# The last layer of a four-layer image kernel turned round: transposes behind the gate, interleaved patches, border columns moved by DMA

## The reference

```python
hidden = conv1x1(x, w_in)                      # 48 -> 288 channels
# patches of 8 x 8: rfft2, times fft_mask, irfft2
hidden = depthwise 3 x 3 (hidden, w_dw)        # 288 channels, zero padding
a, b = split(hidden)                           # 144 and 144
out = conv1x1(gelu(a) * b, w_out)              # 144 -> 48, added to x
```

## Time and profile before

| | |
|---|---|
| time, median of 3 runs | 12465.18 us (12453.49 to 12465.48) |
| profiled execution, span | 12461.3 us (the page has no other time of it) |
| TensorE busy in the span | 97% |
| the last layer | from about 9431 us to the end, 3030 us |

### The profile page before, as it was taken

The page is one execution under the profiler, slowest core; times in us unless marked ns, Lnnn a source line. Parts: engine busy times, 40 slices in busy tenths (PEclk is TensorE's granted clock), DMA queues, the critical chain, the costliest instruction groups (busy, mean ns, idle before and its releaser), DMA issues. The chain is left out here.

```text
span 12461.3 us, 389987 instructions
## 1 busy us (share of the span) xinstructions
PE 12084.7 (97%) x160850; PEld 8648.5 (69%) x160850; DVE 7757.3 (62%) x17493; ACT 5633.1 (45%) x11858; POOL 4999.7 (40%) x4364
## 2 busy tenths in 40 slices
PE   8999999899989999899999999999998999999999
PEld 7877444499977777555555555555557888888887
DVE  0000455444435545788888888888887777777777
ACT  0000111243433333455555555555556777777776
POOL 0000222212420055566666666666663444444444
PEclk9999999999999999999999999999999999999999
DMA  4333465695984587766666666666662222222222
GB/s 142 132 132 132 127 159 154 147 179 89 166 164 146 147 230 199 93 88 87 88 89 88 88 88 88 88 88 87 89 87 67 57 57 57 57 54 56 55 55 52
DMA packets 2289545, 1323.30 MB, mean 106 GB/s; under 512 B 1876085, under 2 KB 2199164, under 8 KB 2202256
## 3 DMA queue, kind: packets, MB, share of 16 engines
q1 hardware_dynamic: 2013196, 1200.80, 49.5%
q10 hardware_dynamic: 275072, 105.14, 3.7%
HBM read 648.82 MB, written 450.45 MB: 88 GB/s over the span
## 5 line engine op out<-in xcount | busy, mean ns | idle before, releaser
L1803 PE MATMUL l_m<-l_wa,l_pix 128*128 128x288 f32 x8192 | 2211.4, 413 | 2.7 <-DVE l_wb L1985 2.7
L1803 PEld LDWEIGHTS l_m<-l_wa,l_pix 128*128 128x128 f32 x8192 | 1475.5, 190 | 688.8 <-issue 361.9
L1659 POOL TENSOR_TENSOR l_qkv<-l_qkv,l_copies 128x576 f32<-128x576 f32 x1024 | 1437.1, 1403 | 631.3 <-DVE l_qkv L1996 621.5
L1649 POOL TENSOR_TENSOR l_pix<-l_raw 128x516 f32<-128x516 f32 x1024 | 1217.1, 1189 | 1042.6 <-DVE l_t L2033 1017.1
L1484 PE MATMUL l1h_ps<-l1h_ring,l1h_w 96*96 96x256 f32 x6120 | 1328.8, 379 | 62.7 <-ACT l1h_ring L1426 60.2
L1484 PEld LDWEIGHTS l1h_ps<-l1h_ring,l1h_w 96*96 96x96 f32 x6120 | 999.8, 163 | 391.5 <-issue 60.4
L2318 PEld LDWEIGHTS l_e<-k_ident,l_turn 128*112 128x112 f32 x9900 | 1069.1, 133 | 173.0 <-issue 110.6
L2318 PE MATMUL l_e<-k_ident,l_turn 128*112 128x128 f32 x9900 | 1158.2, 275 | 11.4 <-ACT l_turn L2403 3.0
L2403 ACT ACTIVATE l_spread<-l_e 112x512 f32<-112x512 f32 (+1 forms) x1584 | 871.7, 569 | 521.4 <-PE l_e L2318 509.5
L1517 DVE SCALAR_TENSOR_TENSOR l1h_ring<-l1h_ps,l1h_bias,l1h_columns 96x256 f32<-96x256 f32 x1020 | 670.4, 657 | 678.4 <-PE l1h_ps L1484 672.7
L517 PE MATMUL l0a_rows<-l0a_x 128*49 128x245 f32 x8144 | 1043.0, 371 | 0.0
(11 more groups left out here) (269 smaller groups left out, 22947.3 us busy)
## 6 DMA issues: line engine op xcount, KB each, us to landing
l0a_x<-x_px_dram SPq DMA_DIRECT2D x128, 1176.0 KB, 5.1
l0b_x<-x_in_dram SPq DMA_DIRECT2D x128, 493.8 KB
l_raw<-l_raw SPq DMA_DIRECT2D x128, 483.6 KB, 7.3
l_raw<-x_dram SPq DMA_DIRECT2D x1270, 48.0 KB, 3.7
l_x<-x3p_dram SPq DMA_DIRECT2D x132, 384.0 KB
l_out<-x_dram SPq DMA_DIRECT2D x528, 96.0 KB, 2.4
out_dram<-l_out SPq DMA_DIRECT2D x132, 384.0 KB, 4.5
x_dram<-l0b_out ACTq DMA_DIRECT2D x256, 193.5 KB, 3.1
```

What stands on the lines that cost most here:

```text
L1649: nc.gpsimd.tensor_tensor(pix[:, n % 2, i, half * HALF:(half + 1) * HALF].rearrange("p (r w) -> p r w", w=PW), in0, in1, op).then_inc(pix_ ...
L1659: nc.gpsimd.tensor_tensor(q, q, copies[:, g % 2, 1:2, :].broadcast_to([128, 2, OUTC]), ALU.add)\
L1803: last = nc.tensor.matmul(bank[i][:, 0:OUTC], pix[:, k, i, first:first + 128], wa[:, b, i, :], start=True, stop=(i in (1, 2)))
```

## The change

Gelu, gate and border adds now work on `turn`, before any transpose: patches on the partitions, positions and channels along the free side. Only the gated product (`gate`) is transposed, 16 times per third, into `rows`; the projection reads `rows`, with four positions of a patch at four places of 32 partitions each. `turn` exists twice.

The two images of a slab are interleaved on the partitions (patch t of image s at 2t + s), so that the neighbour of a patch lies two partitions on. Since neighbours no longer share a partition, `move_edges` sends the outer columns of a third to them, with two transfers of 126 partitions on SyncE's queue; GpSimd clears the two lanes at the seam of the channel halves, waits for the transfers, adds the columns to `turn`, and adds and saves the rows as before. The projection of slab n - 1 is one piece behind convolution 1 of slab n. Channel order in the constants is natural again.

```diff
-            def join(pairs):
-                s = spread[:, pairs]
-                nc.gpsimd.tensor_tensor(s[:, :, 8, :, 0:TX - 1], s[:, :, 8, :, 0:TX - 1], s[:, :, 0, :, 1:TX], ALU.add)
-                nc.gpsimd.tensor_tensor(s[:, :, 1, :, 1:TX], s[:, :, 1, :, 1:TX], s[:, :, 9, :, 0:TX - 1], ALU.add)
...
+                    pool.wait_ge(a_out, conv_at(n, j, COMP))
+                    pool.wait_ge(b_out, conv_at(n, j, COMP))
...
+                    nc.gpsimd.memset(turn[HI:HI + 2, u % 2, 0], 0.0).then_inc(parted, 1)
+                    pool.wait_ge(edge_in[u % 2], 32 * (u // 2) + 32)
...
+                    nc.gpsimd.memset(edge[HI:HI + 2, u % 2, 0], 0.0).then_inc(ended_edge, 1)
+                    nc.gpsimd.tensor_tensor(tile[:, 1:9:7], tile[:, 1:9:7], edge[:, u % 2], ALU.add).then_inc(edged, 1)
...
+            def move_edges(n, j):
+                u = n * 3 + j
+                sp.wait_ge(a_out, conv_at(n, j, COMP))
+                sp.wait_ge(b_out, conv_at(n, j, COMP))
+                if u >= 2:
+                    sp.wait_ge(edged, u - 1)
+                here, there = slice(0, 126), slice(2, 128)
+                for side, column, dst, src in ((0, 9, there, here), (1, 0, here, there)):
+                    if side == 1:
+                        sp.wait_ge(parted, u + 1)
+                    sp.dma_start(edge[dst, u % 2, side, :],
+                                 turn[src, u % 2, column].rearrange("p y g i -> p (y g i)")).then_inc(edge_in[u % 2], 16)
...
+                move_edges(n, 0)
+                move_edges(n, 1)
                 if not first:
-                    store(n)
+                    store(n - 1)
+                move_edges(n, 2)
...
+            def transpose(n, j, ended):
...
+                    if i % 2 == 0:
+                        pe.wait_ge(gate_out, u * 2 + 1 + i // 2)
+                    for k in range(4):
+                        group = 4 * i + k
+                        last = nc.tensor.transpose(bank[:, k * 128:(k + 1) * 128],
+                                                   gate[:, u % 2, 4 * group:4 * group + 4, :].rearrange("p m i -> p (m i)"),
...
+            def project(n, ended):
+                pe.wait_ge(t_out, n * 12 + 12)
...
+                for k in range(6):
+                    j, r = k // 2, k % 2
+                    for m in range(4):
+                        lanes = slice(m * LANE, m * LANE + CH)
+                        for side in range(2):
+                            last = nc.tensor.matmul(e[m][side * HI:side * HI + C, :], wout[lanes, j, r, :],
+                                                    rows[lanes, j, side * 8:(side + 1) * 8, r, :], start=(k == 0), stop=(k == 5),
...
+            def gelu(u, h):
+                if h == 0:
+                    act.wait_ge(edged, u + 1)
+                    act.wait_ge(carried, u + 1)
+                nc.scalar.activation(half(u, 0, h), half(u, 0, h), ACT.Gelu).then_inc(gelu_out, 1)
...
+                        if g < 2 and n > 0:
+                            pe.wait_ge(f_out, n * 4 - 2 + 2 * g)
```

More of the change, by code:

```diff
@@ L2108, in stage_l3 @@
     BANDS = H // 8 + 1
+    N = 2 * BANDS
     CH = C // 2
@@ L2116, in stage_l3 @@
     AB = YR + 3 * COMP
[L2117 to L2125, removed]
+    EDGE = 10 * C
+    LANE = 32
+    GROUPS = PX // 4
     with nc.cleanup_on_exit(), ExitStack() as ctx:
@@ new lines, in slab, with read_y @@
+                transpose(n, 1, last)
+            slabs(slab)
+            transpose(N - 1, 2, True)
+            project(N - 1, True)
+        def read_y(eng, copy, s, n, g, first, done, other, ready):
+            if g == 0 and not first:
+                eng.wait_ge(other, n * AB)
+            eng.wait_ge(done, n * AB + (g + 1))
+            bank = slots[MIX_SLOTS[g % 4]][s]
+            patches = y[:].rearrange("p c (t s) -> p c t s", s=2)[:, :, STARTS[g]:STARTS[g] + SIZES[g], s]
+            copy(patches, bank[:, 0:SIZES[g] * C3].rearrange("p (t c) -> p c t", c=C3)).then_inc(ready, 1)
@@ new lines, in slab @@
+                for g in range(COMP):
+                    read_turn(act, copy, 0, n, 0, g, a_done, a_out)
+                    if g in (0, 2) and not first:
+                        gelu(u - 1, g // 2)
+                if not first:
+                    read_rows(n - 1, 2)
+                for g in range(COMP):
+                    read_turn(act, copy, 0, n, 1, g, a_done, a_out)
+                for h in range(2):
+                    gelu(u, h)
+                read_rows(n, 0)
+                for g in range(COMP):
+                    read_turn(act, copy, 0, n, 2, g, a_done, a_out)
@@ L2439, in _ @@
+                if last:
+                    for h in range(2):
+                        gelu(u + 1, h)
+                else:
+                    for g in range(YR):
+                        read_y(act, copy, 0, n + 1, g, False, a_done, b_done, a_out)
+                        if g in (3, 6):
+                            gelu(u + 1, g // 6)
+                read_rows(n, 1)
             slabs(slab)
-            for piece in range(4):
-                gelu(2 * BANDS - 1, 2, piece)
+            for h in range(2):
+                gelu(N * 3 - 1, h)
@@ L2454, in _ @@
             nc.vector.memset(out[:], 0.0)
+            nc.vector.memset(edge[:], 0.0)
+            nc.vector.memset(gate[:], 0.0)
             dve.wait_ge(wy_done, 1)
@@ L2476, in residual @@
[L2476 to L2482 removed]
+            dve.wait_ge(blank, 1)
+            dve.sem_inc(blank, 1)
+            for g in range(YR):
+                read_y(dve, nc.vector.tensor_copy, 1, 0, g, True, b_done, a_done, b_out)
@@ L2511, in _ @@
-            slabs(slab)
-            for piece in range(4):
-                gated(2 * BANDS - 1, 2, piece)
-            for part in range(2):
-                for s in range(2):
-                    residual(2 * BANDS, part, s)
+                u = n * 3
+                for g in range(COMP):
+                    read_turn(dve, nc.vector.tensor_copy, 1, n, 0, g, b_done, b_out)
+                    if g in (1, 3) and not first:
+                        gated(u - 1, g // 2)
+                for g in range(COMP):
+                    read_turn(dve, nc.vector.tensor_copy, 1, n, 1, g, b_done, b_out)
```

407 lines of the change are left out of this document (166 added, 241 removed).

## The result

| | before | after |
|---|---|---|
| median of 4 runs | 12465.27 us | 12193.41 us (12182.43 to 12203.85) |
| span of the profiled execution | 12461.3 us | 12190.5 us |
| TensorE busy, whole span | 97% | 94% |
| period of a slab | 45.3 us | 41.2 us (forecast 36.9) |

After over before is 0.9786, 95% interval 0.9772 to 0.9799. The kernel is faster by 272 us, where 554 were forecast. The time lies in the range, near its upper end, but the period is further from 36.9 us than the microsecond and a half that the prediction allowed itself.

What follows compares the result with a forecast made beforehand. TensorE's phases were taken as the bound: 32.9 us of work and 4 of waits make a 36.9 us slab instead of 45.3. 12465 - 546 (65 slabs) - 11 (end) + 3 (start) = 11911 us, range 11700 to 12200.

Steps and rivals of the forecast that it cites:

- the sum: TensorE's phases per slab: convolutions 12.9, mixing 8.3, projection 5.4, transposes 6.3, together 32.9 us, 12 less than before.
- rival A: Projection matmuls run four at a time instead of eight: period 40.0 us, time 12110 us; chance 0.12.
- B: Border transfers land late, 5.5 us or more instead of 4.0: 12010 to 12300 us; chance 0.1.
- E: Slower than before: transfers landing after more than 8.6 us make GpSimd's three rounds exceed 45.3 us; 13240 us; chance 0.04.
- D: Waits covered better than walked: TensorE's 32.9 us a slab with 1 of waits, 11715 us; chance 0.1.
- the chain over GpSimd: Border round per third: two memsets 0.5 each, transfers 4, add 2.3, carry 1.85, save 0.85; about 10 us with hand-overs.
- Period 36.9 us, of which 4 are waits: Last layer: one slab takes 36.9 us instead of 45.3, with TensorE waiting for 4 of them.
- The walk: One slab followed in time from convolution 0 through projection, border round, transposes, residual adds and mixing: 36.9 us.
- one for one: Border chain over GpSimd, uncovered once per slab: a longer transfer or add moves the period by as much, at first.
- 12 to `rows`, 0.60 each: ScalarE's 24 evictions to `spread` become 12 copies to `rows` per slab, at 0.60 us each.
- Nothing is added: Convolution and mixing copies out of PSUM: the changed write stride costs no extra time; convolution copies stay at 0.66 us.
- Rival C: VectorE's gates and GpSimd's adds delay each other by 0.5 to 2.3 us per slab: 11945 to 12060 us; chance 0.13.

Runs made afterwards that it cites:

- paced: rows_ts with x, store and residual in 24 pieces of 96 KB, each waiting for one more ScalarE copy: 11917 us.
- no_edge: rows_ts without the border transfers (GpSimd adds zeros; memsets and adds stay): 12146 us.
- quiet: rows_ts without x loads but the first, stores but the last, residual loads but the first, and border transfers: 11841 us.
- rows_ts: The changed kernel with patches left interleaved in `rows`; the residual add reads PSUM in the order that separates the images: 12188 us.
- quiet_thin: quiet with GpSimd's border add, carry and save on one eighth of their elements: 11760 us.
- no_x: rows_ts without the last layer's loads of x after the first: 12004 us.
- no_out: rows_ts without all output stores but the last and all residual loads but the first: 12094 us.
- x_paced: rows_ts with only the loads of x in pieces that wait for copies, store and residual unchanged: 12034 us.
- paced_big: paced with pieces of x and store as 12 whole partitions in packets of 8 KB, same waits: 11988 us.
- pieces: paced with the same 24 small pieces, but none waits for a copy: 11971 us.
- x_late: The changed kernel with the next x loaded behind convolution 1's border transfers instead of ahead of convolution 0's: 12200 us.
- rows_st: The changed kernel with the copy to `rows` writing neighbouring elements and reading every second one: 12187 us.
- x_twice: rows_ts with the same 384 KB copied once more, DRAM to DRAM, behind each load of x: 12168 us.

## Why the prediction was right and wrong

*Right.* TensorE's phases bounded the kernel and shrank as the sum said: projection 5.4 us in one piece, so eight matmuls at a time (rival A falls), transposes 1.9 for 2.1. GpSimd waited 3.1 to 4.8 us for the border transfers (B and E fall; D, at 33.9 us a slab, allowed for 1 us of waits and didn't come), and the chain over GpSimd has its forecast parts.

*Wrong, the step "Period 36.9 us, of which 4 are waits".* The walk knew only waits for semaphores. Missing was one for instructions: TensorE's waits under issue come to 201 / 51 = 3.9 us a slab, against 20.3 / 46 = 0.4 before and 89 / 57 = 1.6 paced. The waits that the walk did have came out smaller: for semaphores TensorE waits 1.7 us a slab instead of 4. The walk also had the border chain uncovered, "one for one"; in no_edge that chain was shorter by 4 us and the period by 0.8 (what the stands of that kernel cover of it isn't known). The rest is TensorE's busy time:

| us a slab, 9600 to 11700 us | forecast | after | paced | quiet |
|---|---|---|---|---|
| TensorE busy | 32.9 | 35.3 | 34.1 | 33.6 |
| waits for semaphores | 4 | 1.7 | 1.0 | 0.5 |
| waits under issue | 0 | 3.9 | 1.6 | 1.7 |

Against quiet, at full clock, TensorE is busy 1.7 us longer. After has half clock for about 2.4 us a slab (an estimate from the mean of 0.97), which accounts for 1.2 of them at most; that share was not measured by itself. With the traffic paced the period is (11845.0 - 9437.4 - 7.5) / 65 = 36.9 us, the number of the forecast. That is partly luck: 1.2 us more of busy time make up for 1.4 less of waits, more than half of the waits that are left are for instructions, and that kernel's copies are those of rows_ts too.

I had priced the transfers by whether they land in time, at a DMA share of 0.24, and never by what they do to TensorE's own queue. The old order loaded x under the transposes; the change put it into a convolution, where TensorE goes through a matmul and a weight load every 23 ns (197 in 4.50 us) and not every 106 (54 in 5.70).

*Wrong, the term "12 to `rows`, 0.60 each".* These copies take 1.14 us. It was a mis-sized term off the critical path, worth nothing measurable by itself. "Nothing is added", said of the other copies, held for the convolution (0.679 us for 500 elements on VectorE, 0.678 before) and not quite for the mixing (432 elements: 0.70 and 0.73 for 0.63).

*Rival C* was half right: the two engines do delay each other, but this isn't what the forecast missed by. In one mixing VectorE and then GpSimd by time:

```profile
11000.07 2.71 DVE L2472 TENSOR_TENSOR l_gate<-l_turn 128x768 f32<-128x768 f32 x1
```

```profile
10999.74 2.23 POOL L2528 TENSOR_TENSOR l_turn<-l_turn,l_edge 128x960 f32<-128x960 f32 x1
11002.05 2.43 POOL L2534 TENSOR_TENSOR l_turn<-l_turn,l_strip 128x768 f32<-128x768 f32 x1
```

A gate of 0.95 us takes 2.71: it begins 0.3 us behind the add and ends 0.8 behind the add's end, by when the carry has begun, and the carry takes 2.43 for 1.82. This agrees with the lockout named in the prediction. Its price lies within the 81 us of quiet_thin.

*How far the cause is shown.* That TensorE stood for its blocks is read from their timing (47 of 49 long stands in after, 71 of 73 in rows_ts); that data held them up is supported by seven kernels in which less or smoother traffic shortened the stands (no_x, no_out, quiet, x_paced, paced_big, pieces, paced). No run delayed a block by itself. In paced only 9 long stands are left, and just 1 of them ends so.

*Open.* The sum under issue doesn't give the time by itself: in x_late, rows_st and rows_ts it changes by 40 to 55 us and the time doesn't, since waits for semaphores change the other way. Why the copy's large packets in x_twice let a block through when those of the loads don't, isn't settled. Nor is it known where the 1.7 us of stands in quiet come from.

## What to carry to other kernels

Where TensorE runs on many small matmuls, its instruction stream is a DMA customer too: issue large loads in small pieces spread over the phase (here 96 KB in packets of 2 KB and less, one piece per copy), and look for idle time under "issue" right behind a high DMA share. An in-order engine should not be given work that waits for a late producer ahead of work that is ready, even if the sum of busy times says that it fits. A copy that becomes faster off the critical path brings nothing, so test which wait it ends before tuning it.

## What the hardware showed

- TensorE's instructions came in blocks of 16 KB, about 253 matmul and weight load records each, and of 49 stands of over 1.5 us in after 47 ended 1.2 to 1.8 us behind the landing of a block.
- A stand of 3.7 us was followed by a granted clock of 0.50 for some 5 us; waits of 3.4 us a slab for a gate went with a mean clock of 0.95 as well.
- A ScalarE copy of 128 x 512 from PSUM took 1.14 us with strided writes of single elements and 0.61 with contiguous ones; VectorE reading PSUM in the interleaved order took 0.683 us per residual add in rows_ts, as without it (0.682).
- Matmuls of 24 rows and 48 columns ran eight at a time, 96 records of them in 5.32 us.
- The same bytes in 24 paced pieces instead of 8 transfers took 270 us off 12188; 768 KB a slab copied besides, in packets of 24 KB, cost nothing (12168).
